# Value products spread 3, 3, 2, 3, 2, 3, 2, 2 over the slots of an octet instead of 3, 3, 3, 3, 3, 3, 2, 0

## The reference, cut to what matters

```
x = x + tanh(g_xattn[0]) * xattn0(layernorm(x), ctx_1024, Wq, Wk, Wv, Wo, bo)
x = x + tanh(g_ffn[0])   * ffn0(layernorm(x), ...)      # quantised, gelu
x = x + tanh(g_xattn[1]) * xattn1(layernorm(x), ctx_1024, mask, ...)
x = x + tanh(g_ffn[1])   * ffn1(layernorm(x), ...)      # spiking, 5 steps
# xattn, per batch row and head:
sim  = (q @ k.T) * scale        # 128 x 77
attn = softmax(sim)
out  = (attn @ v) @ Wo + bo     # summed over 16 heads
```

## Time and profile before

| | us |
|---|---|
| median of 3 runs | 1496.54 |
| lowest and highest | 1496.22, 1498.16 |
| the profiled execution | 1496.88 |
| its span, first to last instruction | 1495.1 |
| PE busy | 1448.0 (97%) |
| PEld busy | 1213.3 (81%) |
| DVE busy | 1081.5 (72%) |
| ACT busy | 892.3 (60%) |
| POOL busy | 635.8 (43%) |

### The profile page before, as it was taken

The page is one execution under the profiler, slowest core; times in us unless marked ns, Lnnn a source line. Parts: engine busy times, 40 slices in busy tenths (PEclk is TensorE's granted clock), DMA queues, the critical chain, the costliest instruction groups (busy, mean ns, idle before and its releaser), DMA issues. The chain is left out here.

```text
span 1495.1 us, 27545 instructions
## 1 busy us (share of the span) xinstructions
PE 1448.0 (97%) x9408; PEld 1213.3 (81%) x9408; DVE 1081.5 (72%) x2327; ACT 892.3 (60%) x1904; POOL 635.8 (43%) x758
## 2 busy tenths in 40 slices
PE   9999999999999999879999999999999999999997
PEld 8888888888888887638978888888888888778886
DVE  4677877676767678899866666676767666776886
ACT  4666666666666654590056666666666666556662
POOL 1343334343333344572023434343333343455885
PEclk9999999999999999999999999999999999999999
DMA  6655534444444432300065444444444444320011
GB/s 222 189 181 161 165 130 152 140 141 145 143 151 133 153 122 87 88 1 1 4 189 164 134 157 132 157 133 161 133 154 133 154 133 151 107 69 8 28 35 44
DMA packets 202787, 182.72 MB, mean 122 GB/s; under 512 B 12368, under 2 KB 201808, under 8 KB 202640
## 3 DMA queue, kind: packets, MB, share of 16 engines
q1 hardware_dynamic: 202080, 180.91, 38.4%
q10 hardware_dynamic: 576, 0.13, 0.1%
HBM read 95.74 MB, written 85.25 MB: 121 GB/s over the span
## 5 line engine op out<-in xcount | busy, mean ns | idle before, releaser
L1131 POOL TENSOR_TENSOR PN<-E,RC 128x512 f32<-128x512 f32 x378 | 331.3, 905 | 491.8 <-DVE RC L1089 491.8
L1038 DVE TENSOR_REDUCE MX<-pS 128x6 f32<-128x462 f32 (+1 forms) x384 | 222.2, 579 | 265.1 <-PE pS L657 265.1
L772 ACT ACTIVATE G<-pP 128x308 f32<-128x308 f32 (+1 forms) x488 | 209.4, 429 | 226.6 <-PE pP L525 226.3
L695 PE MATMUL pO<-work,PT 128*128 128x128 f32 (+1 forms) x2560 | 328.2, 276 | 4.1 <-ACT PT L856 4.1
L657 PE MATMUL pS<-G,XT 128*128 128x462 f32 (+1 forms) x768 | 320.9, 507 | 0.0
L695 PEld LDWEIGHTS pO<-work,PT 128*128 128x128 f32 (+1 forms) x2560 | 307.6, 191 | 8.4 <-issue 6.1
L847 ACT ACTIVATE E<-E 128x462 f32<-128x462 f32 (+1 forms) x384 | 209.6, 546 | 136.1 <-DVE E L1048 128.0
L523 PE MATMUL pP<-Chi,Ahi 128*128 128x308 f32 x496 | 235.1, 474 | 1.4 <-ACT G L772 1.2
L1048 DVE TENSOR_TENSOR E<-pS,MX 128x462 f32<-128x462 f32 (+1 forms) x384 | 223.4, 582 | 8.9
L856 ACT ACTIVATE PT<-pT 128x512 f32<-128x512 f32 (+1 forms) x384 | 200.6, 523 | 29.9 <-PE pT L680 28.5
L1086 DVE TENSOR_REDUCE SM<-E 128x16 f32<-128x1232 f32 (+1 forms) x144 | 184.8, 1290 | 45.1 <-ACT E L847 44.0
(11 more groups left out here) (230 smaller groups left out, 2020.1 us busy)
## 6 DMA issues: line engine op xcount, KB each, us to landing
values<-ST SPq DMA_DIRECT2D x256, 256.0 KB
work<-values SPq DMA_DIRECT2D x512, 128.0 KB
values<-ST SPq DMA_DIRECT2D x64, 208.0 KB
work<-values SPq DMA_DIRECT2D x128, 104.0 KB
C<-in_ctx SPq DMA_DIRECT2D x32, 154.0 KB
X<-in_x SPq DMA_DIRECT2D x16, 256.0 KB, 5.1
out<-s_O SPq DMA_DIRECT2D x16, 256.0 KB, 2.3
work<-in_L_xattn_Wq SPq DMA_DIRECT2D x2, 512.0 KB, 6.0
```

Source lines behind the costliest of these rows:

```text
L695: last = nc.tensor.matmul(pO[:, 0:CH], PT[0:rows, c, :], V[(t - 1) % VRING][0:rows, tile, CH * hh:CH * hh + CH], start=c == 0, stop=c == C ...
L772: return nc.scalar.activation(G[0:live, g % 2, :, head, :], bank[0:live, 0:KEYCOLS].rearrange("p (b k) -> p b k", k=KEYS), ACT.Copy)
L1038: nc.vector.tensor_reduce(MX[:, h0:h1], pS[u][:, 0:(h1 - h0) * KEYS].rearrange("p (h k) -> p h k", k=KEYS), X_AXIS, ALU.max).then_inc(max_ ...
L1131: nc.gpsimd.tensor_tensor(out, e, scale, ALU.mult).then_inc(prob_ready, 1)
```

## The change

PLAN gets other numbers with the same sum of 20. In the slots at positions 0, 1, 3 and 5 there are three value products as before. Positions 2 and 4 have two in place of three, position 6 has two as before, position 7 has two in place of none. The lists of positions 2, 4 and 7 so have six entries, and the places of a list of six. PLACES also gets an entry for a list of five.

```diff
-PLAN = [3, 3, 3, 3, 3, 3, 2, 0]
+PLAN = [3, 3, 2, 3, 2, 3, 2, 2]
@@ attention
-        PLACES = {7: (0, 1, 2, 3, 4, 5, 6), 6: (0, 1, 2, 3, 4, 6), 4: (0, 3, 5, 6), 3: (0, 3, 6), 2: (0, 5), 0: ()}
+        PLACES = {5: (0, 2, 3, 5, 6), 7: (0, 1, 2, 3, 4, 5, 6), 6: (0, 1, 2, 3, 4, 6), 4: (0, 3, 5, 6), 3: (0, 3, 6), 2: (0, 5), 0: ()}
```

## The result

| | before | after |
|---|---|---|
| median of 10 runs, us | 1496.76 | 1500.12 |
| lowest to highest | 1495.97 to 1498.16 | 1498.99 to 1501.71 |
| span of the profiled execution | 1495.1 | 1498.0 |

The ratio is 1.0022 with a 95% interval of 1.0014 to 1.0030: 3.3 us slower, between 2.1 and 4.5. The forecast was 1500.2.

The account below looks back on a forecast made before the run. TensorE was taken as bounding, held at places by ACT's copy of the probabilities behind DVE's chain. Octets gave 3.24 and 0.30, slot 12 0.17: +3.7 us, on the median 1496.54 forecasting 1500.2; range 1496.8 to 1502.0.

Parts of the forecast that it names:

- What bounds the kernel: TensorE's slots, with a chain through DVE and ACT beside them; at position 4 ACT's copy ends at +5.06 whatever TensorE does.
- Position 2: Loses the value at place 5 and becomes slot 30's pattern plus a value: 9.61 to 9.08 us, −0.53, 14 times.
- Position 4: Loses the value at place 5, but weigh 0 then waits for ACT's copy: 9.17 to 8.85 us, −0.32, 14 times.
- rival 1: Position 4 has no stall and saves 0.53 as position 2 does: in all +0.6, 1497.1 us; chance 0.22.
- Slot 12: First layer, DVE late with the next stage's weights: −0.15 there, 0.17 less saved than elsewhere.
- Position 6: The next slot's place 1 gains a value that nothing hides: +0.70 us, 14 times.
- Position 7: A key fills place 2 and the wait for the residual goes: 8.54 to 8.96 us, +0.42, 12 times.
- Slot 55: End of the last octet that makes values, without a context to transpose: 7.85 to 8.15 us, +0.30.
- The sum: +0.27 per full octet times 12, +0.15 per last one times 2, slot 12's 0.17: +3.7 us over both layers.
- Rival 2: A value product is worth its own 0.70 us at any place, also place 5: −4.2, 1492.4 us; chance 0.08.
- Rival 3: At octet boundaries the row fetch waits for value sends: 1.6 us × 14 more, 1522 at worst; chance 0.03.
- Rival 4: Position 7's wait does not go, or ACT is late there too: up to 0.2 × 12 more, 1502.6; chance 0.05.

Follow-up runs that it names:

- e4_copy_first: Changed kernel, but in slots with a list of six ACT copies the first probabilities before the fifth product, TensorE's order untouched: 1495.73 us.
- e1_pos2: Kernel before with one value product moved from position 2 to position 7: 1493.15 us, ratio 0.9976.
- e7_values_late: Changed kernel, in position 7 alone the list is key, key, key, value, key, value, so the last value is at place 6: 1497.33 us.
- e3_late_key: Changed kernel with the fifth product of a list of six at place 5 in place of place 4: 1487.74 us, ratio 0.9943 to before.
- e9_late_key_again: The kernel of e3_late_key unchanged, timed once more: 1488.26 us, ratio 0.9941 to before.
- e2_pos4: Kernel before with one value product moved from position 4 to position 7: 1495.04 us, ratio 0.9991.

## Why the prediction was right

- **What bounds the kernel.** Right, and shown by e4_copy_first: at position 4 TensorE's end is set by DVE's second subtraction, ACT's exponential, ACT's key copy and then the copy of the probabilities, which ended at +5.06 before and after. The 97% said nothing of it.
- **Position 2**, −0.53: measured −0.54, in after and in e1_pos2.
- **Position 4**, −0.32: measured −0.33 (9.19 to 8.85). This is the term in which forecast and rival 1 differ, 2.9 us over 14 slots; rival 1 fell with it. Slot 12, −0.15: measured 10.50 to 10.35.
- **Position 6**, +0.70: measured +0.70.
- **Position 7**, +0.42: measured +0.41. The transposes stood at +3.91, not at the +3.94 read off slot 19. Slot 55, +0.30: measured +0.32.
- **The sum.** +3.7 forecast, +3.15 in both attentions, +3.3 by the ratio. That 1500.2 came within 0.1 us of the median is luck: the sum was too high by 0.4 to 0.6, and the median it was added to (1496.54, three runs) was 0.2 below that of ten. The excess is mostly reading error in the earlier trace rows: with the medians over all slots of both traces in place of one row each, the same sum gives 14 × (−0.537 + 0.700) − 13 × 0.331 − 0.154 + 12 × 0.407 + 2 × 0.32 = +3.35. The remaining 0.2 us belongs to no one position.
- **Rival 2** (a value has one price) fell: a value alone at place 1 costs 0.69 to 0.70, but its absence from place 5 gives back 0.54 and 0.33. The estimate of 0.65 from the Trainium skill ("TensorE: Matmul & The Clock Gate", "Back-to-back issue gap"), whose formula is for a single isolated matmul, is near what a value costs at place 1. What a slot gives back is less where another engine's copy then sets the start of weigh 0.
- **Rival 3** (the boundary) fell, by the trace of after and by e7_values_late. The wait for the sends is there, up to 2.5 us. The Trainium skill ("Perfetto Trace Analysis", "Per-instruction lifecycle") warns of a surprisingly long delay before the semaphore of a write to HBM; here the fetch, which waits for it, began 2.1 to 2.4 us after the last send's issue. The prediction's term for this was too large, 5.1 to 8.7 us. The row is wanted some 14 us after the fetch is issued; the trace shows no landing for the fetch itself.
- **Rival 4** didn't come: the wait before the context transpose went, and ACT's copy of the context wasn't late: from the first transposes to weigh 0 are 331.49 − 330.11 = 1.38 us, as in slot 30, which has no context.
- **The balance of an octet.** A value costs 0.70 us where it is issued without a wait. Positions 2 and 4 gave back 0.54 and 0.33, so 0.16 and 0.37 of theirs turned into new waits before weigh 0 and the slower stretch behind it. Position 7 paid 0.41, so 0.29 less than the price. That is a net: e3_late_key, without the new wait, has 8.78 there, so the new wait costs 8.94 − 8.78 = 0.16 and 0.45 of the product went into the old wait for the residual. 0.53 − 0.29 = +0.24 an octet: with the places of a list of six as they are, spreading the products filled one hole and made larger ones.

## What to carry to other kernels

A product that fills a wait costs less than its own length, and taking it away gives back less: read what starts next and how long after its releaser, and count from there. When work on the bounding engine is spread evenly over steps, check in each step which place becomes empty; here it was the place between the transposes and the products that need ACT's copy, and moving one key there was worth 11 us, more than three times what the spreading cost, and with it the spreading became a gain. So a plan and the places it uses have to be tried together. Start-to-start times by position in a repeated pattern tell a few hundredths of a microsecond, where the page's share shows the same 97%.

## What the runs showed of the hardware

One stretch of TensorE's lower clock between the layers goes with 0.4 to 1.0 us more in an execution of the same work there. The kernel of e3_late_key (first fence) and the same in e9_late_key_again (second), the windows from 600 to 640 us, in the pause between the layers (columns: busy time and instructions of PE, PEld, DVE, ACT, POOL; mean granted clock; DMA share and GB/s):

```profile
600.00:640.00 40.00, 32.55 (x218) 23.03 (x216) 34.96 (x70) 26.61 (x46) 22.85 (x22) 1.00 0.26 68
```

```profile
600.00:640.00 40.00, 33.14 (x220) 24.17 (x219) 33.63 (x69) 25.49 (x43) 22.53 (x23) 0.96 0.26 68
```

A mean of 0.96 is a part of the 40 us at 1.2 GHz and the rest at 2.4. From slot 63 of the first layer to slot 0 of the second the first execution took 177.90 us and the second 178.81. Both attentions, with TensorE busy throughout, took 1108.33 and 1108.36. TensorE was busy for 33 of these 40 us, with gaps, in either; what made the clock fall in one and not in the other wasn't tried. Over all twelve traces, in which this part of the program is the same, the pause took 177.88 to 178.30 us in the eight without such a stretch, 178.67 to 178.83 in the three with one, and 179.14 in e2_pos4, which has a second one in the window from 680 to 690 us (mean 0.83). After's profiled execution had such a stretch there (mean 0.96, 178.83 us) and before's had none (178.30), so 0.5 us of the 2.9 between these two spans is not the change's; 0.8 the other way lies ahead of slot 0 (43.43 after, 44.24 before). The two executions of e3_late_key's kernel differ there too, by 43.41 to 44.27 us. From 6 to 9 us TensorE was busy throughout in both and started 28 matmuls in the first and 21 in the second. That the clock rose later in the second would explain it and is not shown, since the views give no granted clock below 1.00 there.
